# Expert work on Vector and Scalar a gate unit later, each sequence's front begun six units early, the values' transfers issued from Sync

## The reference

```
h  = tok(x)                      # embedding + a spectral code of the one-hot ids
h += attn(layernorm(h))          # 64 summary tokens, windows of 17, 8 heads of 16
h += ffn(layernorm(h))           # router: top 2 of 8 experts, each expert an LSTM

# one expert, one step; xt is the token vector, or zero where the token chose another
gates = xt @ Wi + h @ Wh + b
i_, f_, g_, o_ = split(gates, 4)
c = sigmoid(f_) * c + sigmoid(i_) * tanh(g_)
h = sigmoid(o_) * tanh(c)
y = h @ Wo + bo                  # weighted by the router and summed over both choices
```

## Time and profile before

| | us |
|---|---|
| median of 3 runs (1920.33 to 1920.73) | 1920.38 |
| the profiled execution, its own time | 1918.11 |
| its span, first to last instruction | 1916.3 |
| PE busy | 1729.1 (90%) |
| DVE busy | 1559.5 (81%) |
| ACT busy | 991.9 (52%) |
| up to PE's first gate unit | 120.16 |
| step 0, to the first unit of step 1 | 96.55 |
| steps 1 to 14, to the first unit of step 15 | 1595.70 |
| step 15 and the end | 103.9 |

### The profile page before, as it was taken

The page is one execution under the profiler, slowest core; times in us unless marked ns, Lnnn a source line. Parts: engine busy times, 40 slices in busy tenths (PEclk is TensorE's granted clock), DMA queues, the critical chain, the costliest instruction groups (busy, mean ns, idle before and its releaser), DMA issues.

```text
span 1916.3 us, 25885 instructions
## 1 busy us (share of the span) xinstructions
PE 1729.1 (90%) x9898; PEld 837.6 (44%) x9898; DVE 1559.5 (81%) x2433; ACT 991.9 (52%) x1114; POOL 65.2 (3%) x42
## 2 busy tenths in 40 slices
PE   3457799999999999999999999999999999999998
PEld 2223344444444444444444444444444444444443
DVE  2649698897988889798898988889898888979865
ACT  3234554646555555645545455455555555564544
POOL 1000000000000000000000000000000000000000
PEclk9668899999999999999999999999999999999999
DMA  3113241413314132232313224151331413223221
GB/s 114 20 41 74 57 67 46 77 37 67 63 49 74 39 70 52 52 70 51 67 45 69 51 57 67 44 80 37 63 66 46 76 37 71 53 50 67 55 61 36
DMA packets 318594, 110.95 MB, mean 58 GB/s; under 512 B 240331, under 2 KB 299581, under 8 KB 318471
## 3 DMA queue, kind: packets, MB, share of 16 engines
q1 hardware_dynamic: 202758, 101.96, 23.9%
q10 hardware_dynamic: 115712, 7.34, 3.8%
HBM read 89.84 MB, written 4.74 MB: 49 GB/s over the span
## 4 chain that ended last, share of the span: by engine, by line
PE 40%; DVE 33%; DMA 8%; issue 7%; ACT 5%; ACTq 4%; SPq 1%; POOL 0%; DVEq 0%
PE gates L506 25%; ACTq L619 4%; DVE C L1017 4%; DVE tmp L1007 4%; DMA masks<-mask_scratch 3%; DVE tmp L1013 3%; DMA prod<-in_x_ids 3%; DVE xm L985 3%; PE yp L512 3%; DVE Hs L997 3%; DVE tmp L1028 3%; DVE xn L795 2%; PE FA L447 2%; ACT tmp L655 2%; PE FA L459 2%
## 5 line engine op out<-in xcount | busy, mean ns | idle before, releaser
L655 ACT ACTIVATE tmp<-gates,bias_sb 128x1024 f32<-128x1024 f32 x504 | 557.5, 1109 | 558.6 <-PE gates L506 496.1
L506 PE MATMUL gates<-xm,wi_sb 128*128 128x512 f16 x3024 | 747.3, 384 | 46.2 <-ACT tmp L655 31.0
L506 PE MATMUL gates<-Hs,wh_sb 128*128 128x512 f16 x2880 | 704.4, 381 | 0.0
L506 PEld LDWEIGHTS gates<-xm,wi_sb 128*128 128x128 f16 x3024 | 290.3, 99 | 435.3 <-issue 105.1
L506 PEld LDWEIGHTS gates<-Hs,wh_sb 128*128 128x128 f16 x2880 | 283.2, 98 | 344.3 <-issue 8.0
L662 ACT ACTIVATE tmp<-C 128x1024 f32<-128x1024 f32 x128 | 135.2, 1057 | 226.4 <-DVE C L1017 223.2
L992 DVE SCALAR_TENSOR_TENSOR tmp<-tmp 128x1024 f32<-128x1024 f32 x128 | 155.9, 1218 | 71.8 <-ACT tmp L662 71.8
L1007 DVE SCALAR_TENSOR_TENSOR tmp<-tmp 128x1024 f32<-128x1024 f32 x120 | 144.9, 1208 | 46.4 <-ACT tmp L655 44.9
L985 DVE TENSOR_TENSOR xm<-xs,masks 128x2048 f16<-128x2048 f16 x128 | 155.2, 1212 | 32.7 <-DMA masks<-mask_scratch 32.7
L997 DVE SCALAR_TENSOR_TENSOR Hs<-tmp,Hs 128x1024 f16<-128x1024 f32 x120 | 146.4, 1220 | 37.7 <-ACT Hs L666 36.7
L1013 DVE SCALAR_TENSOR_TENSOR tmp<-tmp,C 128x1024 f32<-128x1024 f32 x120 | 146.4, 1220 | 14.4 <-ACT tmp L655 14.0
(11 more groups left out here) (155 smaller groups left out, 1218.9 us busy)
## 6 DMA issues: line engine op xcount, KB each, us to landing
masks<-mask_scratch SPq DMA_DIRECT2D x128, 256.0 KB, 5.0
roww<-mw_scratch SPq DMA_DIRECT2D x128, 256.0 KB, 4.0
rowk<-mask_scratch SPq DMA_DIRECT2D x128, 128.0 KB, 3.0
diag<-pr SPq DMA_DIRECT2D x64, 112.0 KB, 4.3
diag<-vwin ACTq DMA_DIRECT2D x64, 112.0 KB, 4.8
out_dram<-h SPq DMA_DIRECT2D x16, 256.0 KB, 3.7
C<-in_wi SPq DMA_DIRECT2D x1, 2048.0 KB, 10.9
C<-in_wh SPq DMA_DIRECT2D x1, 2048.0 KB, 15.6
```

Source lines behind the costliest of these rows:

```text
L506: last = mm(gates[:, slot, k * SEQ:(k + 1) * SEQ], w, v, start=(i < K), stop=(i >= len(seq) - K))
L655: A(tmp[:, gate_at(gate, e), :], gates[:, (n - 1) % 2, :], ACT.Tanh, bias=bias_sb[:, e, gate:gate + 1], scale=UNSCALE).then_inc(s_tanh, 1)
```

## The change

Six things are done.

- **Cell work later.** `cell` of expert e-1 runs at g = 0 of expert e (was g = 2 of its own), `cell_tanh` at g = 0 (was g = 3), `hidden` at g = 1 after the front (was g = 0), `input_part` at g = 2 (was 1), `split_hi` at g = 2 (was 0), `hidden_lo` and `chosen` at g = 3 (were 1 and 2), `unit_y` at g = 1 (was 0). An eighth tile in `tmp` keeps two F gates and their cell tanh apart, and `chosen` writes beside its source instead of into `z32`.
- **Fronts six units early.** Units -6 to -1 of a sequence's front run in the last six units of the step before; every piece moves to an earlier unit of its own step. At step 0 these six run at its first unit.
- **First masked input last.** `masked_input` of the next step's expert 0 moves from unit 30, ahead of the rest, to the end of unit 31.
- **Values' transfers from SP**, at unit 7, no longer from ACT.
- **Pairs.** The halves of queries and values are stored as neighbours. Each DMA for `diag` then moves 32x28 runs of 128 bytes and not 32x56 of 64, `v_win` is one 32-bit transpose and not two 16-bit ones, and PE reads `diag` as weights with a step of two elements.
- **Mask rows stored first.** The masks are fetched once the mask rows are stored; the weights' rows are stored and waited for apart, at unit 30.

```diff
-    SP_AT = dict(ids=0, qbd=6, rows=28)
+    SP_AT = dict(ids=-6, qbd=3, vz=7, rows=27, wrow=30)
...
+    EARLY = 6
+    MASKS_AT = 28
...
+    XM_AT = 31
...
+        def run_front(front, t, s):
+            if s == 0 and t == 0:
+                for u in range(-EARLY, 0):
+                    front(u, 1)
+            if s + 1 < STEPS:
+                front(t, s + 1)
+            if s + 2 < STEPS and t >= NG * E - EARLY:
+                front(t - NG * E, s + 2)
...
-                                last = mm(FA[:, r, jj * KB:(jj + 1) * KB], diag[:, qv, j, :, :].rearrange("p g d -> p (g d)"),
+                                last = mm(FA[:, r, jj * KB:(jj + 1) * KB], diag16[:, j, :, qv],
...
-                    for v in (HI, LO):
-                        own = vhl[:, v, :]
...
-                        last = V.transpose(vw16[:, v, :, :], win)
-                    last.then_inc(S["vwin"], 1)
+                    V.transpose(vwj, win).then_inc(S["vwin"], 1)
...
-                    if g == 0 and e:
-                        hidden(s, e - 1)
+                    if g == 0 and e and not first:
+                        cell(s, e - 1)
...
                     if g == 1 and e < E - 1:
                         masked_input(s, e + 1, par, first and e == 0)
-                    if g == 1 and e and not last:
+                    if g == 3 and e and not last:
                         hidden_lo(s, e - 1)
...
-                    if t == XM_AT and not last:
-                        masked_input(s + 1, 0, 1 - par, False)
-                    if g == 2 and e:
+                    if g == 3 and e:
                         chosen(s, e - 1)
...
+                    run_front(lambda u, b: front(u, b, b % 2), t, s)
+                    if g == 1 and e:
+                        hidden(s, e - 1)
...
+                    if g == 2:
                         input_part(s, e, first)
...
+                    if t == XM_AT and not last:
+                        masked_input(s + 1, 0, 1 - par, False)
```

More of the change, by code:

```diff
@@ L53, in lm_tower_kernel @@
     Q_SCALE = 2.0 ** 4
-    SP_AT = dict(ids=0, qbd=6, rows=28)
[L57 to L64, removed]
+    SP_AT = dict(ids=-6, qbd=3, vz=7, rows=27, wrow=30)
+    PE_AT = dict(emb=-3, xT=0, qkv=1, summary=4, window=6, feature=12, values=16, proj=18, x2T=22,
+                 logits=23, maskT=27)
+    ACT_AT = dict(h=-3, xT=0, qkv=1, split=2, summary=6, window=9, pr_hi=13, feature=14, x2T=22,
+                  choice=24, maskT=27)
+    DVE_AT = dict(onehot=-4, moments=-2, xn=-1, pw=2, q_lo=2, kv_lo=3, v_win=4, w_max=5, s_max=7, s_sub=8, w_sum=9,
+                  w_out=10, s_sum=11, s_norm=12, f_max=13, p_lo=14, p_T=15, f_sum=16, f_part=16, attn=17,
+                  moments2=19, xn2=20, x_lo=23, choice1=24, choice2=24, weights=25)
+    EARLY = 6
+    MASKS_AT = 28
     YT_AT, YBACK_AT, YADD_AT = 5, 6, 7
     WT0 = 64
-    XM_AT = 30
+    XM_AT = 31
     ENC0 = 32
@@ L309, in front @@
                     for g in range(NG):
-                        load(diag[32 * g:32 * g + 32, :, :, g, :].rearrange("p v j d -> p (v j) d"),
-                             qz[32 * g:32 * g + 32, :, :, :, :].rearrange("p v j c q -> p (v j) (c q)"), S["qbd"])
+                        load(diag[32 * g:32 * g + 32, :, g, :],
+                             pr[32 * g:32 * g + 32, :].rearrange("p (j d) -> p j d", j=NBLK), S["qbd"])
+                if t == SP_AT["vz"]:
+                    sp.wait_ge(S["vwin"], b + 1)
+                    sp.wait_ge(S["S"], b + 1)
+                    for g in range(NG):
+                        load(diag[32 * g:32 * g + 32, :, g, :], vwj[32 * g:32 * g + 32, :, :], S["vz"])
                 if t == SP_AT["rows"]:
@@ L361, in step @@
                     e, g = t // NG, t % NG
-                    if t == 9 and not first:
+                    if t == 10 and not first:
                         store(s - 1, 1 - par)
-                    if not last:
-                        front(t, s + 1)
+                    run_front(front, t, s)
                     if g == 1 and e < E - 2:
@@ L373, in step @@
                         rows_in(s + 1, 0)
-            for t in range(NG * E):
+            for t in range(-EARLY, NG * E):
                 front(t, 0)
@@ L592, in front @@
                     for c in range(2):
[L593 removed]
+                        last = A(qz[:, :, c, :, HI], qT[:, NW:SEQ].rearrange("p (j q) -> p j q", q=QB), ACT.Copy,
                                  scale=parq[:, c:c + 1])
@@ L1061, in step @@
                         add_y(s - 1, 1 - par)
-                    if not last:
-                        front(t, s + 1, 1 - par)
-                    if g == 1:
+                    run_front(lambda u, b: front(u, b, b % 2), t, s)
+                    if g == 1 and e:
+                        hidden(s, e - 1)
+                    elif g == 1 and not first:
+                        hidden(s - 1, E - 1)
+                    if g == 2:
                         input_part(s, e, first)
-                    if g == 2 and not first:
-                        cell(s, e)
+                    if t == XM_AT and not last:
+                        masked_input(s + 1, 0, 1 - par, False)
             dve.wait_ge(s_zero, 1)
-            for t in range(NG * E):
+            for t in range(-EARLY, NG * E):
                 front(t, 0, 0)
@@ L1081, in _ @@
             run_steps(step)
+            cell(STEPS - 1, E - 1)
             hidden(STEPS - 1, E - 1)
@@ L1107, in step @@
             def step(s, par, first, last):
-                if not last:
-                    for t in range(NG * E):
-                        front(t, s + 1)
+                for t in range(NG * E):
+                    run_front(front, t, s)
             pool.wait_ge(s_zero, 1)
-            for t in range(NG * E):
+            for t in range(-EARLY, NG * E):
                 front(t, 0)
```

111 lines of the change are left out of this document (56 added, 55 removed).

## The result

The change made the kernel slower: a median of 1940.95 us (4 runs, 1940.25 to 1942.0) against 1920.56 of the kernel before beside it, a ratio of 1.0109 with a 95% interval of [1.0095, 1.0123]. The profiled execution took 1942.0 us, its span is 1939.9, 23.6 longer than before. The experiments ran on other chips, where the kernel before took 1914 to 1916 us, so they are compared by their ratios to it; 0.001 is 1.9 us.

What follows compares the result with a forecast made beforehand. PE bounds the kernel, with at most 6.9 us a step to gain. A step becomes 107.1 + 4.8 + 1.7 + 1.9 = 115.5 against 113.98, +21 over 14; with -2, +1.7 and -4.5, +16: 1936 us, range 1897 to 1970.

Steps and rivals of the forecast that it cites:

- The sign and the mechanism: Whole kernel: slower (chance 0.57), because a chain at each step's end makes PE stand and its clock drop.
- Own work: PE's work in one step without waits: 107.1 us, from 108.22 busy less seven tails of 0.16.
- The boundary: End of steps 1 to 13: PE stands 4.8 us for the next masked input; 3.8 at the end of step 14.
- The clock behind it: PE after the boundary stall: 3.5 us at half rate, losing 1.7 us.
- The values' wait: PE at `values`, waiting for the transpose `p_T`: 1.9 us a step, between 0 and 3.
- The step that failed: Reasoning on PE's clock: steady waits of 1.5 us show no drop to half rate.
- First front: Before the first gate unit: shorter waits for `qbd`, `vz` and masks give -4.5 us, between 0 and -6.
- Step 0: First step, bound by DVE: gains 1.0 on the transpose, loses 3 to early pieces; 0, within 2 either way.
- Step 15 and the end: Last step: begins at half clock, adding 1.7 us.
- `vz` off ACT: ACT's issue of the `vz` transfers: removes 3.2 us of ACT a step and most of PE's 2.2 us.
- Weights with a step of two: PE's 168 matmuls with strided weights: cost taken as 0, from below 0 up to 12.6 us a step.
- that rival: Strided weights load at half rate, 25 ns more each: +32 us, 1968; with 32-bit prices about +170; chance 0.14.

Runs made afterwards that it cites:

- the best version: Changed kernel with the first masked input at unit 30, `xn` ahead of `chosen` in unit 31, values and projection a unit later on PE: ratio 0.9565, 1833.34 us.
- the filled stall: Changed kernel with 18 matmuls of 512 columns put before PE's wait for each step's first masked input, from step 1 on: ratio 1.0007.
- both edits together: Changed kernel with the first masked input at the end of unit 30 and the transpose `p_T` a unit earlier: ratio 0.9866.

## Why the prediction was right, and where its terms were off

The sign and the mechanism held, and the time came out 5 us above the 1936. By the spans the change costs 23.6 us where the sum had 16, and that difference is itself made of errors of both signs: steps 1 to 14 came out 28.8 longer and not 19, step 15 with the end 0.4 shorter and not 1.7 longer. That the total is so close is in part luck.

- **Own work**, 107.1: the step's accounts leave 106.9, and the best version takes 107.73 with a wait of 0.88.
- **The boundary**, 4.8: measured 4.74, and 3.72 at the start of step 15 for my 3.8. That the chain makes it is shown by taking it apart (4.74, 3.72, 2.16, none).
- **The clock behind it**, 1.7: measured 1.27 in the steady steps, and nothing at the start of step 15, where I had counted 1.7. That the idle causes it is shown by the filled stall. My reasoning by length, a stall between two idles with a drop, was too simple: idles of 2.16, 2.48 and 3.72 came with either clock.
- **The values' wait**, 1.9: measured 2.10, and the cause, DVE too late for one unit's distance, shown by giving it a unit. The parts held too: from `pw` (1038.00) to the end of `p_T` (1085.81) DVE took 47.8 us for my 47.9, and PE had 49.8 us of work from `qkv` on for my 50.1.
- **The step that failed**: "The steady waits of 1.5 us show no such drop". True in the kernel before, it let me price the values' wait without the clock. Behind that wait the values' unit lost 1.08 us in a steady step, 15 us in all. With 1.27 for 1.7 at the boundary against it, a step is 116.04 and not 115.5.
- **First front**, -4.5: -3.9. The wait for `qbd` fell from 7.32 to 5.54, which is 1.8 for my 2.4. DVE's wait of 1.46 for `vz` is gone, and from the masks' transpose on PE to the first gate unit it is 0.5 shorter, for my 0.6.
- **Step 0**, 0 within 2: -0.9. **Step 15 and the end**, for which I added 1.7: -0.4.
- **`vz` off ACT**, "most of PE's 2.2 us": too much for this edit. By itself it took 12.8 of the 30.1 us, 0.9 a step; the other ACT waits went with the rest of the change. And ACT's 14 waits at `issue` are 42.4 us, 3.0 each; 3.2 is the longest.
- **Weights with a step of two**, 0: right, and that rival is out. PE's weight loads in steps 1 to 14, window and values:

```profile
L470 PEld LDWEIGHTS FA<-xn,diag 128*128 128x128 f16 x1176 | 33.0, 97 | 2.7
...
L482 PEld LDWEIGHTS FA<-vwin,diag 128*128 128x128 f16 x1176 | 31.4, 100 | 34.0 <-DVE vwin L897 34.0
```

They show 97 and 100 ns, and at full clock the 84 narrow matmuls of the values advance PE by 2.1 us as before, 25 ns each. Of the two readings of the Trainium skill that I weighed (TensorE: Matmul & The Clock Gate, section on weight-path perf modes), "packed or strided" is the one that this trace bears out.

The gains that the change was credited with are real but capped: with the boundary's input back in unit 30 the same order runs at 0.9734, and with a unit more for DVE at 0.9565. One instruction's place hid them.

## What to carry to other kernels

Work that the next step cannot begin without should stand ahead of all that waits for another engine; from the end of the last unit but one, add up the chain in front of it, since that sum, less one unit, is the stall of every step. When a wait goes, ask which engine was late: a piece moved inside its list may only pass the wait on, as `p_T` did here, and room for it comes from the engine that waits. And price a wait on PE with the clock behind it, as a chance and not as a threshold, unless other work keeps PE busy.

## What was not expected of the hardware

- The same wait of 1.93 us at the same place had a granted clock of 1.00 behind it in one step and a drop in the next (7 of 14 steps, in two kernels), and the same row of 3.56 us came with a clock of 1.00 in one kernel and 0.64 in another. A clock that falls behind the projection with no idle ahead of it (4 of 14 steps in the kernel before, 7 of 14 in the best version) was not expected either.
- Two different sets of waits gave the same steady step, 116.06 and 116.05 us, and another pair did so too, 112.64 us in their last steps: the masked input behind `hidden_lo`, and both edits together. The clock's losses took up the difference of the waits. It looks like more than chance: in each run the steps only settle at that length (the changed kernel's are 117.50, 116.43, 116.17, 116.08, 116.07, then 116.05 or 116.06), while the stall stays and the loss behind it changes. What sets the length was not tried.
- 18 matmuls whose result nothing uses made a step 1 to 2.5 us shorter.
